# A GRU step loop on one core: the first reset gate of each pass, and what of it stands behind the loop's jump

## The reference

```python
def step(H, xs):                                   # xs = x_t @ W.T + b for the three gates
    xz, xr, xh = xs
    Z = sigmoid(xz + H @ Whz.T + bhz)
    R = sigmoid(xr + H @ Whr.T + bhr)
    H_tilda = tanh(xh + R * H @ Whh.T + bhh)
    H_new = Z * H + (1.0 - Z) * H_tilda
    Y = H_new @ Whq.T + bhq
    return (H_new, Y)
out = x + Ys                                       # 256 steps, one after the other
```

## Time and profile before

| | |
|---|---|
| median of 3 runs | 522.85 us |
| the profiled execution's own time | 525.45 us |
| its span, first to last instruction | 523.7 us |
| mean granted TensorE clock | 0.993 |
| PE busy, PEld busy | 510.9 us, 494.0 us |
| VectorE (DVE) busy, ScalarE (ACT) busy | 316.4 us, 325.0 us |
| one pass of the loop, in the middle | 7.80 us |

### The profile page before, as it was taken

One profiled execution on the slowest core, in us unless ns is written; L12 is line 12 of the kernel. 1 busy time (PEld: TensorE's weight loads), 2 busy tenths in 40 slices (PEclk: granted clock), 3 DMA queues, 4 the chain that ended last, 5 costly groups with the idle time before them and its releaser, 6 DMA issues.

```text
span 523.7 us, 96194 instructions
## 1 busy us (share of the span) xinstructions
PE 510.9 (98%) x44184; PEld 494.0 (94%) x44184; DVE 316.4 (60%) x1929; ACT 325.0 (62%) x1800; POOL 0.2 (0%) x4
## 2 busy tenths in 40 slices
PE   8499999999999999999999999999999999999997
PEld 7399999999999999999999999999999999999997
DVE  1256666666666666666666666666666666666665
ACT  2156666666666666666666666666666666666664
POOL 0000000000000000000000000000000000000000
PEclk9889999999999999999999999999999999999999
DMA  5111111111111112111121111111121121111111
GB/s 176 29 36 50 55 46 53 52 45 55 50 45 55 50 50 53 47 50 55 45 51 54 45 55 50 46 54 50 50 54 47 50 55 46 52 53 45 55 50 51
DMA packets 57736, 27.64 MB, mean 53 GB/s; under 512 B 6784, under 2 KB 56832, under 8 KB 57728
## 3 DMA queue, kind: packets, MB, share of 16 engines
q1 hardware_dynamic: 56880, 26.70, 18.4%
q10 hardware_dynamic: 848, 0.83, 0.5%
HBM read 18.98 MB, written 8.52 MB: 53 GB/s over the span
## 4 chain that ended last, share of the span: by engine, by line
PE 96%; issue 2%; DMA 1%; SPq 0%; DVE 0%; ACT 0%; ACTq 0%; DVEq 0%
PE r_ps L249 34%; PE c_ps L249 28%; PE z_ps L249 23%; PE y_ps L249 11%; DMA whq_sb<-in_whq_dram 1%; SPq L117 0%; SPq L119 0%; SPq L118 0%; SPq L115 0%; DVE o_sb L217 0%; DVE u_sb L235 0%; DVE h_sb L240 0%; DVE rh_sb L230 0%; ACT r_sb L182 0%; ACT z_ps L192 0%
## 5 line engine op out<-in xcount | busy, mean ns | idle before, releaser
L249 PE MATMUL c_ps<-xt_sb,wx_sb 128*32 128x64 f32 (+1 forms) x4104 | 173.9, 225 | 1.8 <-issue 1.8
L249 PE MATMUL z_ps<-xt_sb,wx_sb 128*32 128x64 f32 (+1 forms) x4104 | 164.5, 221 | 0.5 <-issue 0.5
L182 ACT ACTIVATE r_sb<-r_ps 128x32 f32<-128x32 f32 x512 | 91.2, 198 | 109.6 <-PE r_ps L249 101.1
L230 DVE TENSOR_TENSOR rh_sb<-r_sb,h_sb 128x32 f32<-128x32 f32 x512 | 89.8, 192 | 91.1 <-ACT r_sb L182 85.4
L249 PE MATMUL z_ps<-h_sb,whz_sb 128*32 128x32 f32 x8192 | 124.6, 198 | 2.0 <-issue 2.0
L249 PE MATMUL c_ps<-rh_sb,whh_sb 128*32 128x32 f32 x8192 | 123.3, 198 | 2.4 <-issue 2.2
L249 PE MATMUL y_ps<-whq_sb,h_sb 128*32 128x128 f32 x2064 | 113.9, 280 | 0.2 <-DVE h_sb L240 0.2
L249 PEld LDWEIGHTS z_ps<-h_sb,whz_sb 128*32 128x32 f32 x8192 | 109.4, 111 | 2.1 <-issue 2.1
L249 PE MATMUL r_ps<-xt_sb,wx_sb 128*32 128x64 f32 (+1 forms) x4104 | 108.5, 219 | 0.0
L249 PEld LDWEIGHTS z_ps<-xt_sb,wx_sb 128*32 128x32 f32 (+1 forms) x4104 | 102.1, 111 | 0.7 <-issue 0.7
L249 PEld LDWEIGHTS r_ps<-u_sb,whr_sb 128*32 128x32 f32 x5120 | 88.3, 112 | 15.0 <-DVE u_sb L235 15.0
(11 more groups left out here) (29 smaller groups left out, 442.1 us busy)
## 6 DMA issues: line engine op xcount, KB each, us to landing
xt_sb<-in_xt_dram SPq DMA_DIRECT2D x130, 64.0 KB, 1.8
xres_sb<-in_xr_dram SPq DMA_DIRECT2D x130, 64.0 KB, 1.8
out_dram<-o_sb SPq DMA_DIRECT2D x130, 64.0 KB, 1.6
wx_sb<-in_wx_dram SPq DMA_DIRECT2D x3, 256.0 KB, 3.3
whr_sb<-in_whr_dram ACTq DMA_DIRECT2D x1, 256.0 KB, 5.2
whz_sb<-in_whz_dram ACTq DMA_DIRECT2D x1, 256.0 KB, 5.5
whh_sb<-in_whh_dram ACTq DMA_DIRECT2D x1, 256.0 KB, 5.8
whq_sb<-in_whq_dram SPq DMA_DIRECT2D x1, 256.0 KB, 6.8
```

The lines of the kernel that those rows point to most:

```text
L182: nc.scalar.activation(r_sb[:, o], r_ps[:, o, here], ACT.Sigmoid).then_inc(s_r[o], 1)
L230: nc.vector.tensor_tensor(rh_sb[:, k], r_sb[:, k], old[:, k], ALU.mult).then_inc(s_rh[k], 1)
L249: return nc.tensor.matmul(ps, weights, moving, start=start, stop=False, skip_group_check=True, **kw)
```

## The change

Slot 0 gets the blocks zh(0,0) and zh(1,0), both behind the jump (a wait for the new semaphore `s_zh_pass`, then the two blocks), then u(0,0) and u(1,0); its output half 1 is taken from h alone, h(0,1) and h(1,1). That is 6 blocks in place of 5. The block zh(1,0) ahead of `y_piece` in slot 3, and the one before the loop, are gone. VectorE raises `s_zh_pass` for slot 3's zh, by 4 each time, and copies the initial h into `zh_sb` before the loop so that the first pass finds it there. At line 230 slot 0 waits for `s_h[0]` too.

```diff
-AHEAD = [((1, 0),)] + [((0, 0), (1, 0), (1, 1))] * (SLOTS - 1)
+SPLIT = [((0, 0), (1, 0))] + [((0, 0), (1, 0), (1, 1))] * (SLOTS - 1)
 ...
+            nc.vector.tensor_copy(zh_sb[:], h_sb[:, :, SLOTS - 1]).then_inc(s_zh_pass, 1)
 ...
-                        if u > 0:
+                        if u > 0 or k == 0:
                             dve.wait_ge(s_h[k], t + 1)
 ...
-                    nc.vector.tensor_tensor(zh_sb[:], z_sb[:], old, ALU.mult).then_inc(s_zh, 1)
+                    if u == SLOTS - 1:
+                        zh_seen, zh_count = s_zh_pass, t + 2
+                        nc.vector.tensor_tensor(zh_sb[:], z_sb[:], old, ALU.mult).then_inc(s_zh_pass, SLOTS)
+                    else:
+                        zh_seen, zh_count = s_zh, t + 1
+                        nc.vector.tensor_tensor(zh_sb[:], z_sb[:], old, ALU.mult).then_inc(
+                            s_zh, 2 if u == SLOTS - 2 else 1)
 ...
-                    dve.wait_ge(s_zh, t + 1)
+                    dve.wait_ge(zh_seen, zh_count)
 ...
-            for k, o in AHEAD[0]:
-                r_part(0, k, o, h_sb[:, k, SLOTS - 1])
 ...
                     if u == 0:
-                        pe.wait_ge(s_u[1], done)
-                        r_part(u, 1, 0, u_sb[:, 1])
+                        pe.wait_ge(s_zh_pass, done)
+                        for k, o in SPLIT[0]:
+                            r_part(0, k, o, zh_sb[:, k])
+                    pe.wait_ge(s_u[0], done)
+                    r_part(u, 0, 0, u_sb[:, 0])
+                    pe.wait_ge(s_u[1], done)
+                    r_part(u, 1, 0, u_sb[:, 1]).then_inc(s_r_ps[0], 1)
+                    if u == 0:
                         pe.wait_ge(s_h[0], done)
-                        r_part(u, 0, 0, old[:, 0]).then_inc(s_r_ps[0], 1)
                         r_part(u, 0, 1, old[:, 0])
                         pe.wait_ge(s_h[1], done)
                         r_part(u, 1, 1, old[:, 1]).then_inc(s_r_ps[1], 1)
                     else:
-                        pe.wait_ge(s_u[0], done)
-                        r_part(u, 0, 0, u_sb[:, 0])
-                        pe.wait_ge(s_u[1], done)
-                        r_part(u, 1, 0, u_sb[:, 1]).then_inc(s_r_ps[0], 1)
                         r_part(u, 1, 1, u_sb[:, 1])
                         pe.wait_ge(s_h[0], done)
                         r_part(u, 0, 1, old[:, 0]).then_inc(s_r_ps[1], 1)
 ...
-                    pe.wait_ge(s_zh, done)
-                    for k, o in AHEAD[(u + 1) % SLOTS]:
-                        r_part((u + 1) % SLOTS, k, o, zh_sb[:, k])
+                    if u < SLOTS - 1:
+                        pe.wait_ge(s_zh, done)
+                        for k, o in SPLIT[u + 1]:
+                            r_part(u + 1, k, o, zh_sb[:, k])
```

More of the change, by code:

```diff
@@ L108, in gru_kernel @@
         s_zh = sem("s_zh")
+        s_zh_pass = sem("s_zh_pass")
         s_res = sem("s_res")
```

## The result

The changed kernel takes 528.59 us (median of 6 runs, 527.44 to 530.09) beside 523.09 us for the kernel before in runs of the same series. The ratio is 1.0097, 95% interval 1.0078 to 1.0116: slower by 5.1 us (4.1 to 6.1) by this ratio and by 5.5 us by the two medians, where 521.6 was forecast and 525.0 was the end of the range. The profiled execution took 529.33 us, its span is 527.5, and its mean granted clock 0.994.

The account below looks back on a forecast made before the run. TensorE's order was taken as the bound, with the gap at slot 3's jump bound by the jump, u close behind. 63 x (-0.02) + 0.06 = -1.2 us from 522.85 gave 521.6 us, range 519.8 to 525.0.

Parts of the forecast that it names:

- rival 1: The jump keeps its distance from the last output load: 0.02 to 0.04 us a pass slower, up to 525.4 us; chance 0.26.
- F: Start of TensorE's first load behind the jump, in us after 200.00: taken as 0.27 (before 0.40), break-even at 0.30.
- (a): Sequencer runs freely from rh's second half to the jump, at most 6.4 ns an instruction; first load behind it at 0.30.
- (b): Sequencer is held at the wait for zh ahead of the jump; without that wait the first load behind it at 0.22.
- the upper end: First load behind the jump stays 0.35 us after the last output load, so at 0.34; x block at 0.70, 0.04 later.
- The early pass with a gap of 0.14: At half clock the last output load to the first behind the jump took 0.14 us, not 0.35, so 0.35 is no constant.
- The price of a block: A 32-column block on TensorE takes 0.06 us, so two more behind the jump cost 0.12 us.
- the stall of 0.02: In slot 0 behind the jump, TensorE's wait of 0.02 us for h's first half before the change.
- The other name of the semaphore costs nothing: VectorE's semaphore edit, like its other edits, was put at 0, with VectorE 60% busy.
- steps without a jump: Sign: slots 1 and 2 keep 1.93 to 1.95 us; the forecast is wrong if a slot without a jump changed.
- Rival 4: The early stretch at half clock moves; beginning or ending 3 us later costs or gives about 1.3 us; chance 0.05.
- The pass at or above 7.80: Sign: the changed pass should be 7.78 us; at or above 7.80 the forecast is wrong.

Follow-up runs that it names:

- e3: The kernel before with slot 3's zh block put behind the output layer, still ahead of the jump; ratio 0.9993, pass 7.793 us.
- e2: The kernel before with slot 0's gate in six blocks, both zh blocks ahead of the jump; ratio 1.0135, pass 7.880 us.
- e10: The kernel before with 16 tiny TensorE instructions (8 loads, 8 one-column matmuls) added ahead of slot 3's output layer; ratio 1.0137, pass 7.880 us.
- e6: The kernel before with only zh(1,0) moved behind the jump, five blocks kept, VectorE's wait at t + 1; ratio 1.0022, pass 7.805 us.
- e5: The changed kernel with VectorE's slot 3 wait for s_zh_pass at t + 1 in place of t + 2; ratio 1.0093, pass 7.858 us.
- e7: The kernel before with one more VectorE wait, which never holds, on h's first half in slot 3; ratio 1.0103, pass 7.868 us.
- e4: The kernel before with TensorE's loop over 8 slots, 32 passes, halving the jumps; 1433 us, ratio 2.7345.
- e11: The kernel before with 16 tiny TensorE instructions added in slot 1, where no jump follows; ratio 1.0102, pass 7.890 us.
- e9: The kernel before with slot 2's h(0,1) split into zh(0,1) and u(0,1), one block more without a jump; ratio 1.014, pass 7.907 us.

## Why the prediction was wrong

- **The direction was wrong.** Forecast 521.6 with 0.49 for faster; measured 528.6. It was rival 1 (chance 0.26) in kind, and beyond it in size (525.4 at most).
- **F, the step that failed first.** I took 0.27, between (a) 0.30 and (b) 0.22. In the frame of the forecast the first load came at 0.40 - 0.06 = 0.34, the upper end, and with it the forecast's own sum gives 0.70 for the x block, 0.04 a pass slower. Reading (b), a sequencer held at the zh wait, is refuted: the change took that wait from there and e3 moved it behind the output layer, and the jump moved by 0.06 and not at all. Reading (a) had the right kind of cause, the amount that stands ahead of the branch, with 6.4 ns for each instruction. Adding sixteen costs 6.3 ns each (0.10 / 16, e2 and e10). Taking sixteen away gave about 4 ns each in the change (0.06 / 16) and nearly 6 in most passes of e6 (0.09 / 16); the difference between these two is not explained.
- **The early pass with a gap of 0.14 misled me.** It showed that the 0.35 is no constant, which e3 confirms. But it doesn't follow that the jump comes sooner: in e3 the gap shrinks to 0.19 with the jump where it was.
- **The price of a block, the term that was too small.** Two more blocks were to cost 0.10 at the x block (0.36 for six, against 0.26 for four with their stall). They cost 0.13 there (0.40 against 0.27, unrounded) and 0.12 at the update gate and at the first load behind rh. The 0.06 is the pace just behind a pause of TensorE. In the changed kernel the first four blocks keep it (201.30 to 201.54), the two of h take 0.08 each (201.54 to 201.70; the same in e5, where h is 0.07 earlier), and the four blocks of the update gate 0.08 each (0.41 - 0.11 for 31 loads). So the stall of 0.02 that I counted as recovered was lost again. What bounds the slower pace wasn't measured.
- **"The other name of the semaphore costs nothing", a term put at nothing without a reason.** Not the name but the counts did it. The count of the wait put two waits on h: a semaphore instruction more, and h 0.07 late. Alone that is worth 0.068 a pass, 4.3 us over 63 passes and 5.4 us by the ratio (e7), against a forecast of zero. In the change it hides behind the sixth block almost wholly (7.868 against 7.858), so without it the forecast would have been as wrong. The raised counts made zh 0.07 late in slot 2, 0.015 a pass by the steps. I costed VectorE's edits by its 60% share, though the handover from u to h is on the path at each jump.
- **Put together.** At the jump 0.12 for the blocks behind it less 0.06 for the one ahead, 0.053 by the step from slot 3 to slot 0; 0.015 from slot 2 to slot 3; 0.068 a pass.
- **What held.** Two of the three steps without a jump didn't change (0 to 1 and 1 to 2; the windows of the changed kernel below have 1.92 and 1.93 us for slots 1 and 2), the busy shares neither. The step from 2 to 3 did, by 0.015, which the forecast had named as a sign of being wrong. Rival 4 hardly acted: the profiled change reached its first jump 0.8 us earlier, and the pass behind it was 0.25 us longer. The pass at or above 7.80 was named as what would make the forecast wrong, and so it was.
- **The sum.** 63 x 0.068 = 4.3 us, the jumps' rows say 4.4, the ratio 5.1 with 4.1 as its lower end and 6.1 as its upper. Nothing more has to be explained, but nearly 2 us more aren't excluded.

Windows of the changed kernel, slots 1 and 2, cut near the loads of u (columns as in the earlier trace rows):

```profile
203.30:205.22 1.92, 1.92 (x187) 1.92 (x180) 1.38 (x10) 1.14 (x7) 0.00 (x0) 1.00 0.11 33
205.22:207.15 1.93, 1.93 (x185) 1.93 (x178) 1.06 (x9) 1.38 (x8) 0.00 (x0) 1.00 0.29 69
```

## What to carry to other kernels

Work moved behind a loop's jump must be counted twice: what it frees ahead of the jump (here 0.06 to 0.09 us for 16 instructions) and what it adds behind it. A block that was split to fit two sides costs its weight loads and matmuls again, however few columns they have. A price read just behind a stall is the lowest one (0.06 us for a block here, 0.08 to 0.11 elsewhere). A gap that follows a jump isn't spare room unless the jump itself can start sooner. When an edit changes a semaphore, or only a count, look at what the waiting and the raising instruction carry: here a second wait, or a raise by more than one, was another instruction on the engine. On the tight handover from u to h such a wait alone cost as much as the whole change did.

## What the runs showed of the hardware that I had not expected

- Where two waits fell on one instruction of VectorE, one became a semaphore instruction (21 ns), and the instruction behind it starts 0.10 us after its producer's end in place of 0.04 (0.103 to 0.105 in each of 59 passes in the middle of e7, 0.033 to 0.035 in 60 of the kernel before).
- Where an instruction of VectorE raised a semaphore by 2 or 4 in place of 1 (zh in slots 2 and 3), its wait stood on a semaphore instruction (21 ns) too, and it started 0.10 us behind its producer's end in place of 0.03.
- TensorE's compare and branch starts 0.34 us ahead of the first load behind the jump in every run but e4, though the last load ahead of the jump stands 0.19 (e3) to 0.40 us (e10) ahead of it.
- 8 loads and 8 one-column matmuls ahead of the jump shift it as much as a block of 32-column tiles in float32, 0.10 us (e10, e2); in a slot without a jump they cost 0.090 us a pass against 0.107 for a block (e11, e9).
- A TensorE loop body of about 1,380 recorded instructions costs 208 ns at its jump, one of about 2,760 costs 3.7 us there and stalls some twelve times a pass, 523.9 us against 1433 in all, at a granted clock of 0.756.
